# Upsampling matmuls on eight tiles of 32x64 round six banks, and the summing one stage further ahead

## What is computed

```python
pre_up = gate[:, :, None, None] * x + x
up = jnp.repeat(pre_up, 2, axis=1) * w_up[None, :, None, None]
return _bilinear_up_x2(up) + sx
```

```python
out = input + bias[None, :, None, None]
upf = up_filter * UP
out = _sep_upfirdn(out, upf, UP, 1, UP_PAD)                 # both axes x2: 256x256
out = jax.nn.leaky_relu(out, NEG_SLOPE) * FLRELU_SCALE
out = _sep_upfirdn(out, down_filter, 1, DOWN, DOWN_PAD)     # both axes /2: 128x128
```

## Time and profile before

| | |
|---|---|
| median of 3 runs | 7928.65 us (7927.54 to 7929.11) |
| profiled execution | 7925.67 us |
| its span, first to last instruction | 7923.9 us |
| TensorE matmul / weight load | 7411.7 us (94%) / 6562.6 us (83%) |
| VectorE | 6318.9 us (80%) |
| ScalarE | 4073.0 us (51%) |
| GpSimd | 2543.3 us (32%) |
| mean granted TensorE clock | 0.969 |

### The profile page before, as it was taken

One profiled execution on the slowest core, in us unless ns is written; L12 is line 12 of the kernel. 1 busy time (PEld: TensorE's weight loads), 2 busy tenths in 40 slices (PEclk: granted clock), 3 DMA queues, 4 the chain that ended last, 5 costly groups with the idle time before them and its releaser, 6 DMA issues.

```text
span 7923.9 us, 374577 instructions
## 1 busy us (share of the span) xinstructions
PE 7411.7 (94%) x151493; PEld 6562.6 (83%) x151493; DVE 6318.9 (80%) x12643; ACT 4073.0 (51%) x8046; POOL 2543.3 (32%) x3076
## 2 busy tenths in 40 slices
PE   7999966069999999999999999999999999999999
PEld 3444441059999999999999999999999999999999
DVE  8999942878888888888888888888888888888887
ACT  0000002346666666666666666666666666666666
POOL 0000000024444444444444444444444444444443
PEclk9999978579999999999999999999999999999999
DMA  7777714013333333333333333333333333333333
GB/s 307 313 306 316 310 58 180 0 55 91 92 90 92 90 93 90 93 90 92 91 92 90 92 91 92 91 91 92 91 92 91 92 90 93 90 92 91 93 90 87
DMA packets 1253328, 925.41 MB, mean 117 GB/s; under 512 B 175312, under 2 KB 1224912, under 8 KB 1234384
## 3 DMA queue, kind: packets, MB, share of 16 engines
q1 hardware_dynamic: 1243920, 890.10, 34.7%
q10 hardware_dynamic: 9344, 34.61, 1.6%
HBM read 621.50 MB, written 303.04 MB: 117 GB/s over the span
## 4 chain that ended last, share of the span: by engine, by line
PE 79%; DVE 0%; POOL 0%; DMA 0%; ACT 0%; issue 0%; POOLq 0%; DVEq 0%
PE bank L991 38%; PE bank L980 30%; PE bank L985 9%; PE bank L1044 2%; DVE x_sum L1135 0%; DMA img<-in_x 0%; DMA low<-conv_dram 0%; ACT slope_t L1091 0%; DVE leaky L1152 0%; POOL low_f L959 0%; POOL img L947 0%; ACT dn L1117 0%; POOL low_d L956 0%; POOL lift L962 0%; ACT low_v L1100 0%
## 5 line engine op out<-in xcount | busy, mean ns | idle before, releaser
L1152 DVE SCALAR_TENSOR_TENSOR leaky<-bank,slope_t 128x512 f32<-128x512 f32 x4096 | 2637.2, 685 | 575.6 <-ACT slope_t L1091 511.2
L1091 ACT ACTIVATE slope_t<-bank 128x512 f32<-128x512 f32 x4096 | 2219.8, 597 | 1697.8 <-PE bank L985 1697.8
L980 PE MATMUL bank<-up_t,up 64*128 64x133 f32 x16384 | 2186.2, 273 | 1.4 <-DVE leaky L1152 1.2
L985 PE MATMUL bank<-up_t,up 64*128 64x133 f32 x16384 | 2186.3, 273 | 0.0
L991 PE MATMUL bank<-down_t,leaky 128*64 128x67 f32 x65536 | 2086.2, 222 | 0.0
L980 PEld LDWEIGHTS bank<-up_t,up 64*128 64x128 f32 x16384 | 2009.0, 187 | 2.4 <-DVE leaky L1152 1.0
L985 PEld LDWEIGHTS bank<-up_t,up 64*128 64x128 f32 x16384 | 2006.3, 187 | 0.0
L991 PEld LDWEIGHTS bank<-down_t,leaky 128*64 128x64 f32 x65536 | 1999.0, 137 | 0.1
L1144 DVE COPY up<-bank 128x512 f32<-128x512 f32 x2048 | 1318.7, 685 | 626.6 <-PE bank L985 626.6
L956 POOL TENSOR_TENSOR low_d<-low_v 128x252 f32<-128x252 f32 x512 | 310.9, 607 | 4023.6 <-ACT low_v L1100 4023.6
L985 PE MATMUL bank<-up_t,x_sum 64*128 64x133 f32 x8192 | 1521.0, 299 | 0.0
(11 more groups left out here) (154 smaller groups left out, 3468.3 us busy)
## 6 DMA issues: line engine op xcount, KB each, us to landing
img<-in_x SPq DMA_DIRECT2D x1024, 256.0 KB, 2.8
out<-res SPq DMA_DIRECT2D x1024, 256.0 KB, 2.2
rows_in<-in_x SPq DMA_DIRECT2D x48, 4224.0 KB, 13.9
rows_in<-in_x SPq DMA_DIRECT2D x16, 4096.0 KB, 13.9
conv_dram<-conv ACTq DMA_DIRECT2D x64, 512.0 KB, 4.1
xb<-conv_dram SPq DMA_DIRECT2D x8, 4096.0 KB, 13.3
low<-conv_dram SPq DMA_DIRECT2D x512, 64.0 KB, 2.3
xx<-conv_dram SPq DMA_DIRECT2D x2, 2048.0 KB, 9.9
```

What stands on the lines that cost most here:

```text
L980: return pe.matmul(acc[:, 0:UP_REACH], src, up_t[0:HALF, 0:UP_REACH], start=first, stop=False, skip_group_check=True)
L985: return pe.matmul(acc[:, UH - UP_REACH:UH], src, up_t[HALF:P, UH - UP_REACH:UH], start=first, stop=False, skip_group_check=True)
L1091: nc.scalar.activation(slope_t[e][i][:], u2_acc[e][i][:], ACT.Copy, scale=SLOPE * GAIN).then_inc(slope_out, 1)
L1152: v.scalar_tensor_tensor(out=leaky[1 - m % 2][:, e, i].rearrange("p k w -> p (k w)"), in0=u2_acc[e][i][:], scalar=GAIN, in1=slope_t[e][i][ ...
```

## The change

- The up matmuls are cut into 32 rows by 64 columns of weights: four row tiles (rt) times two column tiles (`rise`). A row tile of 32 reaches 69 or 74 output columns (`UP_REACH`). A slot has 96 of them instead of 24.
- They go in 12 steps round six banks. `ITEMS` lists the six accumulators, two of first up and four of second up, each with two halves. In step t, row tile rt works on half-item (t - 3 rt) mod 12, so that no two row tiles write one bank. Before each step from the third on, TensorE waits on `up_step` until the step before the last is complete. The waits for the sources and for the emptied banks (`u1_out0`, `u1_out1`, `leaky_out`, `res_ready`) stand at each item's first use, all of them in steps 0 and 1.
- b1 becomes two column tiles with 128 rows (rows 64 to 127 of `low` are zero), moves behind the up steps and writes bank 7. `low` is one buffer instead of two. TensorE's order is: 12 steps, b1 in every second slot, first_down(0), second down (now in bank 1), first_down(1), which in a slot with b1 waits for `b1_out`.
- ScalarE takes over one of the two copies of u1 and does: slopes (0,0), (0,1), (1,0), copy of u1, slope (1,1), low_v, res, two copies of dn. VectorE does: the other copy of u1, four leaky, x_sum. All start once the slot's twelfth step is complete.
- x_sum and the bias run two slots ahead, b1 and widening four; the loads move with them.
- TensorE's loop holds two slots (`PE_STEP`, eight images) instead of four.

The diff, cut to its core (16 columns of indentation are taken off):

```diff
-UP_REACH = 2 * HALF + 5
+T = 32
+NT = P // T
+UP_REACH = [(max(0, 2 * T * r - 5), min(UH, 2 * T * (r + 1) + 5)) for r in range(NT)]
...
-low = [sb(f"low{i}", [HO, LOWS, WO]) for i in range(2)]
+low = sb("low", [P, LOWS, WO])
...
-d2_acc = bank[0]
-b1_acc = bank[6][:, 0:LOWS * WO]
+d2_acc = bank[1]
+b1_acc = bank[7][:, 0:LOWS * WO]
...
+ITEMS = ((1, 0), (2, 0, 0), (2, 1, 1), (2, 0, 1), (2, 1, 0), (1, 1))
+STEPS = 2 * len(ITEMS)
...
-FIRST, LAST = -2, PAIRS + 2
+FIRST, LAST = -4, PAIRS + 2
 STEP = 4
-LOOP0, LOOP1 = STEP, PAIRS - STEP
...
+PE_STEP = 2
+LOOP0, LOOP1 = STEP, PAIRS - 2 * STEP
...
     if u is not None:
         return (u + k) // of * per
-    return r * (STEP // of * per) + (m + k) // of * per
+    return r * (step // of * per) + (m + k) // of * per
...
-        done = cnt(u, r, m, 2, of=2)
+        g = cnt(u, r, m, 6, per=2)
+        done = cnt(u, r, m, 6, of=2)
...
+        if has(u, -2):
             add_bias(u, r, m)
-        if m % 2 == 0 and has(u, -2):
+        if m % 2 == 0 and has(u, -4):
             widen(u, r, m)
...
-    def upper(acc, src, first):
...
+    pe.wait_ge(padded, 1)
...
-    def first_up(e, i, p, half, first):
...
+    def rise(acc, src, rt, first):
+        a, b = UP_REACH[rt]
+        for c in range(2):
+            mm = pe.matmul(acc[cols(c), a:b], src[:, cols(c)], up_t[T * rt:T * (rt + 1), a:b],
+                           start=first, stop=False, skip_group_check=True)
+        return mm
...
         mm.then_inc(d1_mm, 1)
     def slot(u, r, m):
-        group = m % 2 == 0 and has(u, -2)
+        group = m % 2 == 0 and has(u, -4)
         p = m % 2
-        if has(u, 0):
...
+        used = set()
+        for t in range(STEPS if has(u, 0) or has(u, 1) else 0):
+            if t >= 2:
+                pe.wait_ge(up_step, cnt(u, r, m, 0, per=STEPS, step=PE_STEP) + (t - 1))
+            for rt in range(NT):
+                at = (t - 3 * rt) % STEPS
+                item, half = ITEMS[at // 2], at % 2
+                rows = slice(T * rt, T * (rt + 1))
+                if item[0] == 1 and has(u, 0):
+                    i = item[1]
+                    if not used & {(1, 0), (1, 1)}:
+                        pe.wait_ge(x_summed, cnt(u, r, m, 1, step=PE_STEP))
+                    if item not in used and i == 0 and after(u, 1):
+                        pe.wait_ge(u1_out0, cnt(u, r, m, 0, step=PE_STEP))
+                    if item not in used and i == 1 and after(u, 1):
+                        pe.wait_ge(u1_out1, cnt(u, r, m, 0, step=PE_STEP))
+                        if after(u, 4):
+                            pe.wait_ge(res_ready, cnt(u, r, m, -3, step=PE_STEP))
+                    mm = rise(u1_acc[i][:, half * UH:(half + 1) * UH], x_sum[p][rows, half, i, :], rt, item not in used)
+                    used.add(item)
+                if item[0] == 2 and has(u, 1):
+                    e, i = item[1:]
+                    if item not in used:
+                        if i == 0:
+                            pe.wait_ge(u1_out0, cnt(u, r, m, 0, step=PE_STEP))
+                        else:
+                            pe.wait_ge(u1_out1, cnt(u, r, m, 0, step=PE_STEP))
+                        if after(u, 2):
+                            pe.wait_ge(leaky_out, cnt(u, r, m, -2, per=4, step=PE_STEP) + (2 * e + i + 1))
+                    mm = rise(u2_acc[e][i][:, half * UW:(half + 1) * UW], up1[1 - p][rows, i, e, half * P:(half + 1) * P],
+                              rt, item not in used)
+                    used.add(item)
+            mm.then_inc(up_step, 1)
         if group:
-            pe.wait_ge(low_loaded[(m // 2 + 1) % 2], cnt(u, r, m, 2 + 4, per=16, of=4))
+            pe.wait_ge(low_loaded, cnt(u, r, m, 4 + 2, per=16, of=2, step=PE_STEP))
+            if u is not None and -2 <= u < 4:
+                pe.wait_ge(b1_out, cnt(u, r, m, 4, of=2, step=PE_STEP))
             if after(u, 3):
-                pe.wait_ge(d1_out, cnt(u, r, m, -3, per=2) + 1)
...
+                pe.wait_ge(d1_out, cnt(u, r, m, -2, per=2, step=PE_STEP))
+            for c in range(2):
+                mm = pe.matmul(b1_acc[cols(c)], const("lin")[:, cols(c)], low[:].rearrange("p c w -> p (c w)"),
+                               start=True, stop=True)
+            mm.then_inc(b1_mm, 1)
+        if has(u, 2):
+            pe.wait_ge(leaky_out, cnt(u, r, m, -1, per=4, step=PE_STEP))
+            if after(u, 3):
+                pe.wait_ge(d1_out, cnt(u, r, m, -3, per=2, step=PE_STEP) + 1)
+            first_down(0, p)
         if has(u, 3):
-            pe.wait_ge(d1_out, cnt(u, r, m, -2, per=2))
+            pe.wait_ge(d1_out, cnt(u, r, m, -2, per=2, step=PE_STEP))
             if has(u, 0):
-                pe.wait_ge(u1_out, cnt(u, r, m, 0, per=2) + 1)
+                pe.wait_ge(u1_out1, cnt(u, r, m, 1, step=PE_STEP))
             elif after(u, 4):
-                pe.wait_ge(res_ready, cnt(u, r, m, -3))
+                pe.wait_ge(res_ready, cnt(u, r, m, -3, step=PE_STEP))
             for e in range(2):
                 for i in range(2):
                     for j in range(2):
...
                                       dn1[1 - p][:, e, j, i, cols(c)], j, e == i == j == 0)
             mm.then_inc(d2_mm, 1)
         if has(u, 2):
-            pe.wait_ge(leaky_out, cnt(u, r, m, -1, per=4))
+            if after(u, 3):
+                pe.wait_ge(d1_out, cnt(u, r, m, -2, per=2, step=PE_STEP))
             if group:
-                pe.wait_ge(b1_out, cnt(u, r, m, 4, of=2))
-            for e in range(2):
-                first_down(e, p)
-    schedule(pe, slot)
+                pe.wait_ge(b1_out, cnt(u, r, m, 6, of=2, step=PE_STEP))
+            first_down(1, p)
+    schedule(pe, slot, PE_STEP)
...
     def slot(u, r, m):
         p = m % 2
-        if m % 2 == 0 and has(u, -2):
-            act.wait_ge(b1_mm, cnt(u, r, m, 4, of=2))
-            if after(u, 0):
-                act.wait_ge(lifted, cnt(u, r, m, 2, of=2))
+        if has(u, 1):
+            act.wait_ge(up_step, cnt(u, r, m, 1, per=STEPS))
+            slope(u, r, m, 0, 0)
+            slope(u, r, m, 0, 1)
+            slope(u, r, m, 1, 0)
+        if has(u, 0):
+            act.wait_ge(up_step, cnt(u, r, m, 1, per=STEPS))
+            nc.scalar.activation(up1[p][:, 0].rearrange("p e h -> p (e h)"), u1_acc[0][:], ACT.Copy).then_inc(u1_out0, 1)
+        if has(u, 1):
+            slope(u, r, m, 1, 1)
+        if m % 2 == 0 and has(u, -4):
+            act.wait_ge(b1_mm, cnt(u, r, m, 6, of=2))
+            if after(u, -2):
+                act.wait_ge(lifted, cnt(u, r, m, 4, of=2))
             nc.scalar.activation(low_v[:].rearrange("p c w -> p (c w)"), b1_acc, ACT.Copy).then_inc(b1_out, 1)
-        if has(u, 1):
-            act.wait_ge(u2_mm, cnt(u, r, m, 0))
-            slope(u, r, m, 0)
         if has(u, 3):
             act.wait_ge(d2_mm, cnt(u, r, m, -2))
             if after(u, 5):
                 act.wait_ge(res_stored[1 - p], cnt(u, r, m, -3, per=16, of=2))
             nc.scalar.activation(res[1 - p][:].rearrange("p i w -> p (i w)"), d2_acc[:], ACT.Copy).then_inc(res_ready, 1)
-        if has(u, 1):
-            slope(u, r, m, 1)
         if has(u, 2):
             for e in range(2):
                 act.wait_ge(d1_mm, cnt(u, r, m, -2, per=2) + (e + 1))
...
 @block.vector
 def _(v):
+    v.memset(low[HO:P], 0.0).then_inc(padded, 1)
...
     def slot(u, r, m):
-        if has(u, -1):
...
         if has(u, 0):
-            v.wait_ge(u1_mm, cnt(u, r, m, 1))
...
+            v.wait_ge(up_step, cnt(u, r, m, 1, per=STEPS))
+            v.tensor_copy(up1[m % 2][:, 1].rearrange("p e h -> p (e h)"), u1_acc[1][:]).then_inc(u1_out1, 1)
         if has(u, 1):
...
+        if has(u, -2):
+            n = (m + 2) % STEP
+            v.wait_ge(lifted, cnt(u, r, m, 2 + 2, of=2))
+            v.wait_ge(biased, cnt(u, r, m, 3))
...
+            ins.then_inc(x_summed, 1)
```

More of the change, by code:

```diff
@@ L827, in resample @@
                 img_loaded = [sem(f"img_loaded{i}") for i in range(2)]
-                low_loaded = [sem(f"low_loaded{i}") for i in range(2)]
+                low_loaded = sem("low_loaded")
                 res_stored = [sem(f"res_stored{i}") for i in range(2)]
@@ L835, in resample @@
                 x_summed = sem("x_summed")
[L836 to L840, removed]
+                padded = sem("padded")
+                up_step = sem("up_step")
+                u1_out0 = sem("u1_out0")
+                u1_out1 = sem("u1_out1")
                 slope_out = sem("slope_out")
@@ L922, in slot @@
                     def slot(u, r, m):
-                        if m % 2 == 0 and has(u, -4):
+                        if has(u, -3):
+                            load_img(u, r, m)
+                        if m % 2 == 0 and has(u, -6):
                             load_low(u, r, m)
-                        if has(u, -2):
-                            load_img(u, r, m)
                         if has(u, 3):
                             store(u, r, m)
```

(22 more changed lines are left out.)

99 lines of the change are left out of this document (25 added, 74 removed).

## The result

The changed kernel takes 8644.86 us (median of 4 runs, 8635.38 to 8647.87) against 7928.09 for the kernel before: ratio 1.090, 95% interval 1.088 to 1.092. That is 717 us slower, where 360 us slower was forecast: the time lies inside the stated range (7880 to 8800), at nearly twice the forecast loss. The profiled execution has a span of 8644.1 us.

The account below looks back on a forecast made before the run. TensorE's stream was taken to bound the kernel. Slots of 6.04 us without b1 and 6.86 with it make 12.90 against 12.20; 0.70 x 512 = 360 us more gives 8290 us, range 7880 to 8800.

Parts of the forecast that it names:

- The sign: Whole kernel: the change makes it slower, by 360 us; chance of slower 0.85.
- the bound: Kernel before: TensorE's stream alone sets the period, 6.10 us a slot, with everything that leaves PSUM hidden.
- the two stalls: Last down group waits for low_v in b1 slots, about 0.75 us; step 1 waits for leaky in others, about 0.55.
- U: Start of a slot's last up record on TensorE, the zero point from which the forecast counts times.
- two steps: Up phase: the chain from release to release takes 0.11 + 0.05 + 0.29 = 0.45 us for each two steps.
- the leaky wait: Slot without b1: step 1 waits for the fourth leaky, seen at 3.70 us; 2.34 us from there to the last record.
- the forecast's own band: Up phase: a step between 0.205 and 0.25 us, for 8050 to 8640 us; chance 0.70.
- rival D: TensorE's sequencer, issuing up matmuls, is the bound; 8690 us at 0.020 us a matmul; chance 0.15.
- The step's lower bound, 0.13: Up phase: two passes of 74 columns without a pause, the tiles' own rate, make 0.13 us a step.
- Rival B: Up phase: the wait between steps is nearly free, steps take 0.13 us, time 7315 us (-614); chance 0.10.
- The operations before step 1 is out: TensorE's loop end: four more register operations add 0.5 us, costed at nothing; without cover 0.4 us in two slots.
- The ten operations for up_step: Up phase: ten more register operations per slot, 0.095 us each plus eight matmuls a step; at the low half hidden behind 0.22.

Follow-up runs that it names:

- e6: Kernel before the change, with b1 split over both row halves of the array as two side-by-side matmuls: 7819.80 us, ratio 0.9863.
- e4: Changed kernel without the step waits on up_step; each row tile adds into its own bank, the sum over row tiles left out: 7864.45 us.
- e5: Changed kernel with one more register operation and a long satisfied wait ahead of each step's wait on up_step: 8751.88 us.
- e11: Changed kernel with each step's two bank-continuing row tiles issued first and setting the release, the wait only before the other two: 8178.77 us.
- e10: e4 with only the first two row tiles in the loop, 48 up matmuls instead of 96: 7321.41 us.
- e2: Changed kernel with only the first two row tiles in the loop's up phase, all step waits kept: 8690.80 us.
- e13: e12 with ScalarE's slope (1,1) moved ahead of its copy of u1: 7886.43 us.
- e9: Changed kernel with the earlier 64x128 up tiles put back, second halves waiting on two separate releases: 8485.46 us, ratio 1.070.
- e12: e11 with ScalarE's low_v copy moved ahead as in e1: 7866.73 us, ratio 0.9921.
- e1: Changed kernel with ScalarE's low_v copy moved from behind slope (1,1) to behind slope (0,1): 8363.36 us.
- e8: Changed kernel with the earlier 64x128 up tiles put back, second halves waiting on one common release behind both first halves: 8833.31 us.

## Why the prediction came out as it did

**Right.** The sign, the bound and the two stalls. TensorE alone bounds the kernel before (e6: 109 us saved, 107 expected). Up starts 4.37 us after U in b1 slots (4.34 forecast); leaky(1,1) lets step 1 go at 3.73 (3.70); the low_v stall is 0.76 (0.76), released by the copy that the forecast named. Down's records are still 0.029 us apart.

**The term that was mis-sized: two steps, 0.45 us forecast, 0.503 measured.** Its first half was right (0.11 + 0.05 against 0.16). The second, from the last record's start to the next load, I took from the earlier trace rows as 0.34 and cut to 0.29 because the record is 0.05 us shorter. It is 0.34 here as well, for 69 columns as for 133. Twelve steps take 2.87 and not 2.52; from the leaky wait on it is 2.58 and not 2.34. With 0.03 each for the two start points that makes 0.35 + 0.24 + 0.06 = 0.65 us in two slots, 333 us: 8290 + 333 = 8623 of the 8645. The trace accounts for both parts. Of the 0.35, five pairs of 0.053 make 0.27, and the last two steps 0.08: 0.35 us where I had put 0.27, because step 11 starts 0.19 us after step 10. Of the 0.24, four pairs make 0.21, and 0.02 is a slip: 0.41 + 4 x 0.45 + 0.15 is 2.36, not the 2.34 of the forecast. The row had measured what I wanted, start to start; the correction was the error.

**How good the number was.** Steps of 0.25 us were the upper end of the forecast's own band. Its bracket is miscounted (12 x 0.02 x 1024 is 246, not 215), but its "340 us up" for 0.25 gives 8630, near what was measured. The time alone couldn't have told this from rival D, which at 0.020 us a matmul gave 8690. It took e4, e5 and e11.

**The step's lower bound, 0.13, was too low for eight tiles.** e4 shows 0.18. Rival B at 7315 wasn't to be had: without waits it is 7864, a gain of 64 us and not 614. The Trainium skill, "TensorE: Matmul & The Clock Gate", The mechanism, has a weight load overlap running matmuls only where the row group differs, which would fit a floor for each row group, as e10's 0.132 for a step of four tiles may be; it doesn't give the 0.18, and no run here tests it.

**Rival D.** By my working it started to decide at 0.016 us a matmul, and e4 excludes only more than 0.022, so e4 alone doesn't refute it. What does is that one more operation a step costs 0.010 us and not 0.095 (e5), that half the matmuls save a tenth (e2), and that the same matmuls and operations in another order save 466 us (e11). The 62 ns a matmul that I quoted from the Trainium skill ("TensorE: Matmul & The Clock Gate", Wait — 56ns, not 53.3ns?) are for hardware decoding off. They don't describe these runs: 96 matmuls in 2.16 us (e4) are 0.022 us each.

**Costed at nothing.** The operations before step 1 is out: right for the changed kernel, where the last of them comes 3.57 us after U in a slot without b1 and the leaky wait ends at 3.73. Where that cover goes (e13), by the traces they hold the up phase by 0.20 and some 0.3 us in two slots; the forecast had put 0.4 on it. The ten operations for up_step: no room is left for them in the pair, 0.163 + 0.340 is all of its 0.503. The res wait: covered in the changed kernel by the leaky wait, bare in e9. "ScalarE and VectorE busy time unchanged" was wrong. ScalarE took over 1024 copies of 0.62 us, which the forecast's own order of its operations held (4073 to 4511 us). VectorE, with 1024 copies fewer, rose from 6319 to 6660 us, by x_sum (below). Neither is on the path at 6.77 us a slot; at 6.0 (e4, e12) VectorE is close to it.

**What the moves cost.** I had put the loss on the steps and stalls together. With the wide tiles in the new order (e9) 557 of the 717 us are there already, about 164 of them by a res wait that the changed kernel hides. All banks are handed over at the end of the up phase, and low_v stands behind five other operations; of this e1 prices the second (282 us), the rest is argued.

## What to carry to other kernels

Smaller tiles shift the bound from the array's stream to the hand-over of the banks: price it as the start-to-start time from a row that already shows such a wait, uncorrected, and ask which matmuls of a step need the wait at all (e11). Then see what the new order releases late: where one more accumulator shares a bank with the end of a phase, the copy that frees it belongs early in its engine's queue. On a kernel whose main engine is never idle, a small saving on that engine (e6) pays in full, while a large one that brings waits (this change) may not.

## What the runs showed of the hardware

**A wait of TensorE on its own matmul** costs 0.34 us from the start of the last record to the next weight load, for 69 columns (4006.66 to 4007.00 in the changed kernel) as for 133 (7910.43 to 7910.77 in the kernel before; taking one such wait out of each slot gained 0.34 us from e8 to e9).

**Operations for wait values.** Where nothing hides them they stand about 0.1 us apart on TensorE's sequencer, and TensorE's matmuls behind such a wait can't start earlier (e13). While TensorE still works through matmuls issued before, they cost nothing (e11).

**VectorE against GpSimd.** In the kernel before, x_sum (two of its inputs in SBUF) takes 0.344 us each time. One stage earlier it meets GpSimd's widening. The timelines of the changed kernel, VectorE, then GpSimd:

```profile
4005.26 1.13 DVE L1162 SCALAR_TENSOR_TENSOR x_sum<-lift,coef,img 128x128 f32<-128x128 f32 x4
```

```profile
4012.22 1.20 DVE L1162 SCALAR_TENSOR_TENSOR x_sum<-lift,coef,img 128x128 f32<-128x128 f32 x1
```

```profile
4012.06 1.22 POOL L969 TENSOR_TENSOR low_f<-low_d,cst 128x504 f32<-128x504 f32 x1
4013.35 1.11 POOL L972 TENSOR_TENSOR lift<-low_f,low_v 128x504 f32<-128x504 f32 x1
```

Four x_sum take 1.13 us with GpSimd idle; beside low_f a single one takes 1.20, as long as GpSimd's operation. Of 588 x_sum in 1000 us, the 296 away from the widening mean 0.345 us and the 292 beside it 0.82. The leaky operations, with one input in PSUM, keep their 0.686. The Trainium skill, "SBUF — State Buffer", Who interferes with whom, says that a VectorE instruction with two SBUF inputs contends with a GpSimd one that reads SBUF, and calls the ports that they share an exclusive lock. The trace agrees: the slowed x_sum lasts as long as GpSimd's instruction.

**The clock.** In e2 TensorE is busy in 994 of 1000 us, and yet its granted clock falls from 1.00 to 0.50 at the end of an up phase of 48 small matmuls, in every second slot, and is back at 1.00 some 3 us later. With 96 of them (the changed kernel) it stays at 1.00, and so it does in e10, with the same 48 but no step waits, in up phases of 1.59 us where e2's last 2.60 and 2.78. So the count alone isn't it; no run separates what is.
